# A counting stage of one-hot matrix products: three banks for the counts, one-hots by half batches, a tile's linear products spread over seven slots

## What is computed

```
edge_index = jnp.stack([src, dst])
x = x + _L0_gnn_ref(_layernorm(x), edge_index, L0_gnn_Ws, L0_gnn_Wb, L0_gnn_a_w, L0_gnn_a_b)
x = x + _L0_ffn_ref(_layernorm(x)[None], L0_ffn_Wg, L0_ffn_bg, L0_ffn_We, L0_ffn_be)[0]
x = x + _L1_gnn_ref(_layernorm(x), edge_index, L1_gnn_W, L1_gnn_b)
x = x + _L1_ffn_ref(_layernorm(x)[None], L1_ffn_Wr, L1_ffn_br, L1_ffn_W1, L1_ffn_b1, L1_ffn_W2, L1_ffn_b2)[0]
```

```
Wx = x @ Ws[h] + Wb[h]
s = Wx[v_tgt] @ a_w[h, :d] + Wx[v_src] @ a_w[h, d:] + a_b[h]
alpha = _segment_softmax(leaky_relu(s, 0.2), v_tgt, n)
out_h = segment_sum(alpha[:, None] * Wx[v_src], v_tgt)
```

## Time and profile before

| | us |
|---|---|
| median of 3 runs | 609.81 |
| lowest and highest | 604.17, 610.58 |
| the profiled execution: its time | 610.48 |
| the profiled execution: its span | 608.7 |

### The profile page before, as it was taken

The page is one execution under the profiler, slowest core; times in us unless marked ns, Lnnn a source line. Parts: engine busy times, 40 slices in busy tenths (PEclk is TensorE's granted clock), DMA queues, the critical chain, the costliest instruction groups (busy, mean ns, idle before and its releaser), DMA issues.

```text
span 608.7 us, 11871 instructions
## 1 busy us (share of the span) xinstructions
PE 519.3 (85%) x4561; PEld 369.7 (61%) x4562; DVE 458.2 (75%) x863; ACT 333.0 (55%) x644; POOL 72.5 (12%) x83
## 2 busy tenths in 40 slices
PE   2879999887657998999889478996999965999995
PEld 1856666554457888889777344543466635776762
DVE  6788887788589999996888837785656554687771
ACT  5355555455597999997465433344322217665640
POOL 3000000000000000000000300223132430042252
PEclk9769999999969999999999878999899976899999
DMA  7950000002001111110000067000001039366211
GB/s 190 357 209 1 2 2 1 1 2 90 3 1 44 45 46 45 49 42 2 2 1 2 0 218 283 1 0 0 4 20 54 36 105 381 136 207 208 79 49 47
DMA packets 25304, 45.11 MB, mean 74 GB/s; under 512 B 6961, under 2 KB 7205, under 8 KB 25248
## 3 DMA queue, kind: packets, MB, share of 16 engines
q1 hardware_dynamic: 23264, 39.16, 18.9%
q0 software_dynamic: 1952, 5.18, 2.3%
q10 hardware_dynamic: 32, 0.01, 0.0%
HBM read 33.23 MB, written 11.95 MB: 74 GB/s over the span
## 4 chain that ended last, share of the span: by engine, by line
PE 49%; DVE 25%; issue 13%; ACT 7%; POOL 3%; DMA 1%; ACTq 1%; POOLq 0%; DVEq 0%
PE bank L1300 8%; PE bank L1633 7%; PE bank L1621 6%; PE bank L1364 6%; PE bank L1323 4%; DVE work L1013 4%; PE bank L1371 3%; PE bank L1543 2%; ACT mid L523 2%; PE bank L1478 2%; PE bank L1465 2%; PE bank L1278 2%; DVE rings L1013 2%; POOL row L467 2%; DVE work L971 1%
## 5 line engine op out<-in xcount | busy, mean ns | idle before, releaser
L908 DVE TENSOR_TENSOR big<-mid 128x3072 f16<-128x3072 f16 (+3 forms) x52 | 88.3, 1743 | 9.1 <-PE bank L1371 9.0
L1364 PE MATMUL bank<-big 128*128 128x160 f16 x552 | 72.8, 245 | 13.4 <-ACT mid L523 4.7
L1465 PE MATMUL bank<-big,work 128*128 128x130 f16 x1080 | 67.2, 223 | 12.1 <-DVE work L1013 11.8
L1465 PEld LDWEIGHTS bank<-big,work 128*128 128x128 f16 x1080 | 63.5, 99 | 14.9 <-DVE work L1013 8.1
L1364 PEld LDWEIGHTS bank<-big 128*128 128x128 f16 x552 | 44.3, 105 | 35.1 <-issue 28.0
L1543 PE MATMUL bank<-mid 128*128 128x512 f16 x200 | 47.6, 389 | 3.3 <-POOL mid L441 3.3
L523 ACT ACTIVATE mid<-bank 128x160 f32 x92 | 27.9, 303 | 40.5 <-PE bank L1371 40.4
L625 ACT ACTIVATE mid<-aux,small 128x1280 f16<-128x1280 f32 x36 | 47.4, 1350 | 1.5 <-DVE work L1013 1.1
L1478 PE MATMUL bank<-big,mid 128*128 128x260 f16 x400 | 47.1, 275 | 0.1
L523 ACT ACTIVATE big<-bank 128x160 f32 x92 | 27.9, 303 | 31.6 <-PE bank L1371 29.1
L1478 PEld LDWEIGHTS bank<-big,mid 128*128 128x128 f16 x400 | 38.2, 96 | 7.5 <-issue 0.3
(11 more groups left out here) (293 smaller groups left out, 1100.1 us busy)
## 6 DMA issues: line engine op xcount, KB each, us to landing
big<-in_L_ffn_W SPq DMA_DIRECT2D x10, 1024.0 KB, 9.4
mid<-in_L_ffn_W SPq DMA_DIRECT2D x6, 1024.0 KB, 13.5
xperm_scratch<-work SPq DMA_DIRECT2D x1, 5753.0 KB, 19.4
aux<-thr_scratch SPq DMA_DIRECT2D x8, 640.0 KB, 3.8
aux<-xperm_scratch SPq DMA_DIRECT2D x8, 523.0 KB, 3.9
row<-in_x SPq DMA_DIRECT2D x1, 2304.0 KB
aux<-in_L_gnn_Ws SPq DMA_DIRECT2D x4, 256.0 KB, 4.4
work<-in_L_gnn_W SPq DMA_DIRECT2D x1, 1024.0 KB, 14.8
```

The costliest lines, as they stand in the source:

```text
L908: return V.tensor_tensor(out.rearrange("p c (v two) -> p c v two", two=2), values.rearrange("p (v two) -> p v two", two=2).unsqueeze(1).to ...
L1364: mm(bank[k % 2][:, 0:RW], L_ring[:, slot, k * CH + j, :], R_ring[:, slot, k * CH + j, :], start=j == 0, stop=False)
L1465: ins = mm(acc_region(h, t), weighted[i % NC][:, t * P:(t + 1) * P], VP[:, s, part, h, :, :].rearrange("p b f -> p (b f)"), start=False, s ...
```

## The change

- `count_bank`: the counts of a batch go through three banks, 0, 1 and 7 by (8b + k) % 3, where they went through 0 and 1. count(k+1) then waits for the write of pair k-2, which merge(k) ahead of it has waited for already. merge(k) still waits for the write of pair k-2, since the count matrices are two as before. (Passes after the first, which this input does not have, keep two banks.)
- Bank 7 is given up by the others: tile transposes use bank 6 alone, and `tile_T` of tile t waits for the low half of tile t-1. The weight transposes use banks 6 and 2, and the thresholds 3, 4, 5.
- `half_onehots`: the one-hots of a batch are made in four instructions (1536, 1920, 1536, 1920 elements) where there were two. The first half needs pairs 0 to 3 of batch b-2 counted, the second all eight. `onehots` goes up by 4 behind each half.
- `LIN_SLOTS`: the twelve products stand at k = 0, 1, 3, 4, 5, 6, 7 as 1, 2, 2, 2, 1, 2, 2; none at k = 2, where the transposes are.
- On DVE, `evac_a` goes from the end of iteration t+4 to between the halves of iteration t+5, and `xT_low` from the start of iteration t+4 to the end of t+3.

```
--- before.py
+++ after.py
@@ -54,6 +54,7 @@
 
 
 BEGIN = {1 + t: t for t in range(T)}
+LIN_SLOTS = ((0,), (1, 2), (), (3, 4), (5, 6), (7,), (8, 9), (10, 11))
 B_GW = max(BEGIN) + 2
 B_CS = B_GW + K
 EPS = 1e-5
@@ -291,6 +292,13 @@
                 skip_runtime_bounds_check_because="the groups' windows come from targets in 0 to NP, clipped to the last window")
             return at
 
+        def count_bank(base, k):
+
+            return bank[(0, 1, 7)[(base + k) % 3]] if isinstance(base, int) else bank[k % 2]
+
+        def gw_bank(k):
+            return bank[(6, 2)[k % 2]]
+
         def counts_at(at, k):
 
             return (C, C2)[k % 2][:, :, bass.ds(at, WN)]
@@ -520,7 +528,7 @@
                 for k in range(LB):
                     if not isinstance(base, int):
                         a.wait_ge(sem("counted"), base + (k + 1))
-                    ins = act(counts_at(at[k], k), bank[k % 2][:, 0:RW].rearrange("p (d s) -> p s d", s=T), ACT.Copy)
+                    ins = act(counts_at(at[k], k), count_bank(base, k)[:, 0:RW].rearrange("p (d s) -> p s d", s=T), ACT.Copy)
                     if isinstance(base, int):
                         ins.wait_op(sem("counted"), base + (k + 1), "sem-ge")
                     ins.then_inc(sem("written"), 1)
@@ -576,7 +584,7 @@
                         t = BEGIN[b - 1]
                         if t >= 2:
                             a.wait_ge(sem("linA"), t - 1)
-                        ln_copy(t, bank[6 + t % 2], xTs[:, t % 2, 0, :, :])
+                        ln_copy(t, bank[6], xTs[:, t % 2, 0, :, :])
 
                 write_batch(b * LB, at[b], middle)
                 if b == 0:
@@ -589,11 +597,11 @@
                 if b - B_GW in range(K):
                     k = b - B_GW
                     a.wait_ge(sem("gwT_psum"), k + 1)
-                    act(gWT[:, 0, k, :], bank[6 + k % 2][:, :], ACT.Copy, scale=WS).then_inc(sem("weight_hi"), 1)
+                    act(gWT[:, 0, k, :], gw_bank(k)[:, :], ACT.Copy, scale=WS).then_inc(sem("weight_hi"), 1)
                 if b == B_CS:
                     for i, n in enumerate((4, 4, 2)):
                         a.wait_ge(sem("thrT_psum"), i + 1)
-                        act(thrT[0:H, i * 512:i * 512 + n * P], bank[5 + i][0:H, 0:n * P], ACT.Copy).then_inc(sem("thrT_ready"), 1)
+                        act(thrT[0:H, i * 512:i * 512 + n * P], bank[3 + i][0:H, 0:n * P], ACT.Copy).then_inc(sem("thrT_ready"), 1)
             a.wait_ge(sem("exp_in"), 1)
             act(B12[:, 0, :, :], d1t, ACT.Exp)
             act(B12[:, 1, :, :], d1t, ACT.Exp, scale=SLOPE)
@@ -914,6 +922,14 @@
                 onehot(L_ring[:, slot, :, :], iota_lo, loT[:, bass.ds(off * CH, LC), :], LC, P)
                 onehot(R_ring[:, slot, :, :], iota_q, qT[:, bass.ds(off * CH, LC), :], LC, RW).then_inc(sem("onehots"), LB)
 
+            def half_onehots(b, half):
+                n = LC // 2
+                c = slice(half * n, (half + 1) * n)
+                e = slice(b * LC + half * n, b * LC + (half + 1) * n)
+                at_least(v, "counted", (b - 2) * LB + (half + 1) * (LB // 2))
+                onehot(L_ring[:, b % 2, c, :], iota_lo, loT[:, e, :], n, P)
+                onehot(R_ring[:, b % 2, c, :], iota_q, qT[:, e, :], n, RW).then_inc(sem("onehots"), LB // 2)
+
             def first_onehots():
                 n = LC // 4
                 for q in range(4):
@@ -927,16 +943,18 @@
                     v.wait_ge(sem("ld_x"), 64)
                 if b in BEGIN:
                     ln_stats(BEGIN[b], x[:, BEGIN[b], :])
-                if b - 3 in BEGIN:
-                    t = BEGIN[b - 3]
-                    xT_low(t, bank[6 + t % 2], xTs[:, t % 2, :, :, :])
                 if b - 2 - B_GW in range(K):
                     k = b - 2 - B_GW
                     v.wait_ge(sem("weight_hi"), 2 + k + 1)
-                    V.scalar_tensor_tensor(gWT[:, 1, k, :], bank[6 + k % 2][:, :], WS, gWT[:, 0, k, :],
+                    V.scalar_tensor_tensor(gWT[:, 1, k, :], gw_bank(k)[:, :], WS, gWT[:, 0, k, :],
                                            ALU.mult, ALU.subtract).then_inc(sem("weight_lo"), 1)
                 if b:
-                    onehots(b * LB, b * LB, b % 2, 2)
+                    half_onehots(b, 0)
+                    if b - 4 in BEGIN:
+                        evac_a(BEGIN[b - 4])
+                        if BEGIN[b - 4] == T - 1:
+                            scores()
+                    half_onehots(b, 1)
                 else:
                     first_onehots()
                     passes()
@@ -950,10 +968,9 @@
                                            Wa[:, 0, :, :].rearrange("p k c -> p (k c)"), ALU.mult, ALU.subtract).then_inc(sem("weight_lo"), 1)
                 if b - 1 in BEGIN:
                     ln_scale(BEGIN[b - 1])
-                if b - 3 in BEGIN:
-                    evac_a(BEGIN[b - 3])
-                    if BEGIN[b - 3] == T - 1:
-                        scores()
+                if b - 2 in BEGIN:
+                    t = BEGIN[b - 2]
+                    xT_low(t, bank[6], xTs[:, t % 2, :, :, :])
             exponents()
             v.wait_ge(sem("npass_ready"), 1)
             n = v.value_load(npass[0:1, 0:1], min_val=1, max_val=MAXPASS)
@@ -1310,19 +1327,20 @@
             mm(bank[5][0:NG, 0:1], tri[0:NG, 0:NG], grp[0:NG, 2:3], start=True, stop=True)
             mm(bank[4][0:1, NPAIR:NPAIR + 1], ones[0:NG, 0:1], grp[0:NG, 2:3], start=True, stop=True).then_inc(sem("rb_psum"), 1)
 
-            def lin_a(t, k):
-                if k == 0:
+            def lin_a(t, j):
+                k, i = divmod(j, len(PASSES))
+                xp, wp = PASSES[i]
+                if j == 0:
                     if t == 0:
                         pe.wait_ge(sem("weight_lo"), 2)
                     pe.wait_ge(sem("xT_ready"), t + 1)
                     if t >= 2:
                         pe.wait_ge(sem("evacA"), t - 1)
-                for i, (xp, wp) in enumerate(PASSES):
-                    xt = xTs[:, t % 2, xp, k, :]
-                    start, stop = i == 0 and k == 0, i == 2 and k == K - 1
-                    mm(bank[2 + t % 2][:, :], xt, W016[:, wp, k, :], start=start, stop=stop)
-                    ins = mm(bank[4 + t % 2][:, 0:2 * H], xt, Wa[:, wp, k, :], start=start, stop=stop)
-                if k == K - 1:
+                xt = xTs[:, t % 2, xp, k, :]
+                last = j == K * len(PASSES) - 1
+                mm(bank[2 + t % 2][:, :], xt, W016[:, wp, k, :], start=j == 0, stop=last)
+                ins = mm(bank[4 + t % 2][:, 0:2 * H], xt, Wa[:, wp, k, :], start=j == 0, stop=last)
+                if last:
                     ins.then_inc(sem("linA"), 1)
 
             def second_weights(k):
@@ -1330,10 +1348,12 @@
                 if k == 0:
                     pe.wait_ge(sem("xT_ready"), T)
                     pe.wait_ge(sem("ld_gw"), 16)
+                if k == 1:
+                    pe.wait_ge(sem("evacA"), T - 1)
                 if k >= 2:
                     pe.wait_ge(sem("weight_lo"), 2 + k - 1)
                 for o in range(K):
-                    ins = nc.tensor.transpose(bank[6 + k % 2][:, o * P:(o + 1) * P], gW[:, o, k * P:(k + 1) * P], ident[:, :])
+                    ins = nc.tensor.transpose(gw_bank(k)[:, o * P:(o + 1) * P], gW[:, o, k * P:(k + 1) * P], ident[:, :])
                 ins.then_inc(sem("gwT_psum"), 1)
 
             def thresholds():
@@ -1341,7 +1361,7 @@
                 pe.wait_ge(sem("weight_lo"), 2 + K)
                 for i, n in enumerate((4, 4, 2)):
                     for q in range(n):
-                        ins = nc.tensor.transpose(bank[5 + i][0:H, q * P:(q + 1) * P], thr[:, 4 * i + q, :], ident[:, :])
+                        ins = nc.tensor.transpose(bank[3 + i][0:H, q * P:(q + 1) * P], thr[:, 4 * i + q, :], ident[:, :])
                     ins.then_inc(sem("thrT_psum"), 1)
 
 
@@ -1359,16 +1379,16 @@
 
             def count(base, slot, k):
                 pe.wait_ge(sem("onehots"), base + (k + 1))
-                at_least(pe, "written", base + (k - 1))
+                at_least(pe, "written", base + (k - 2) if isinstance(base, int) else base + (k - 1))
                 for j in range(CH):
-                    mm(bank[k % 2][:, 0:RW], L_ring[:, slot, k * CH + j, :], R_ring[:, slot, k * CH + j, :],
+                    mm(count_bank(base, k)[:, 0:RW], L_ring[:, slot, k * CH + j, :], R_ring[:, slot, k * CH + j, :],
                        start=j == 0, stop=False)
 
             def merge(base, k, at):
 
                 if not isinstance(base, int):
                     pe.wait_ge(sem("written"), base + k - 1)
-                ins = mm(bank[k % 2][:, 0:RW].rearrange("p (d s) -> p s d", s=T), ident16[:, :], counts_at(at[k], k),
+                ins = mm(count_bank(base, k)[:, 0:RW].rearrange("p (d s) -> p s d", s=T), ident16[:, :], counts_at(at[k], k),
                          start=False, stop=True)
```

(9 more changed lines are left out.)

77 lines of the change are left out of this document (48 added, 29 removed).

## The result

| | us |
|---|---|
| before, median of 4 runs beside it | 608.46 (604.17 to 610.58) |
| after, median of 4 runs | 589.74 (588.83 to 591.3) |
| ratio, with its 95% interval | 0.9704, 0.9643 to 0.9764 |
| the profiled execution: time, span | 591.3, 589.5 |

The change makes the kernel about 3% faster. Of all runs in this document one, among the ten of the variant with two banks, fell in a slower state of the chip, and its row leaves it out. I set the trace of after against the same three landmarks as the forecast.

The account below looks back on a forecast made before the run. PE, waiting for its two count banks, was taken to bound the counting stage, with DVE following. Gains of 5.4 and 6.4 us, 11.8 off the profiled 610.5, gave 598.7, stated as 598.5; range 594.5 to 604.5.

Parts of the forecast that it names:

- Batches 0 to 2 I leave as they are: Start of the counting stage, up to batch 3's first merge: no gain entered in the sum.
- 1 or 2 us more: Batches 1 to 3: possible extra gain, as half of batch 2's one-hots no longer wait for batch 0's end.
- Products: Batches 3 to 12, which carry linear products: from 69.8 to 64.4 us, 5.4 us less.
- 0.93 is lost, all in the five slots that have no product: PE in batches 3 to 12: of the 7.04 us period, 0.93 goes to counts waiting for ScalarE to empty the bank.
- DVE follows PE there: Batches 3 to 12: DVE's 6.38 us of work plus a 0.67 wait for PE's products, so PE sets the period.
- These cost nothing while DVE is ahead: Moved `evac_a` and `xT_low` on DVE: no cost; if DVE is not ahead, 6.52 a batch instead of 6.46.
- Rest: From batch 12's last merge to the last count write: from 48.7 to 42.3 us, 6.4 us less.
- The 0.45: Pair loop: at most 0.45 us from the write's start to the merge, giving 0.79 for two pairs, 0.40 for one.
- A: Pair loop not shortened: pairs stay at 0.495 us, PE decides again, 4 us of gain lost, 603 us; chance 0.12.
- B: DVE's fixed part per instruction is 0.16 us: iterations 6.70, one-hots 4.06, 3.4 us lost, 602 us; chance 0.10.
- C: DVE's lead too short: PE waits for `xT_low` every batch, nothing gained with products, 604 us; chance 0.10.
- D: PE's clock falls to 1.2 GHz from its short waits in batches 13 to 22: slower, 616 us; chance 0.06.

Follow-up runs that it names:

- the second pair of series: The changed kernel, unedited, run again beside the kernel before: median 590.59 us, ratio 0.9723.
- the whole hand-over: Changed kernel with its four one-hot instructions handed over together and waiting together for all of batch b-2: 595.8 us, ratio 0.9836.
- the late weight halves: Changed kernel with DVE's four low halves of the third layer's weights moved to the end of iterations 14 to 17: 590.97 us, ratio 0.9735.
- whole one-hots: Changed kernel with DVE's weight halves late, thresholds one batch later, and two one-hot instructions a batch except in batches 2 and 22: 589.91 us, ratio 0.9722.

## Why the prediction missed

**The start (5.2 us, forecast 0): the largest part of the miss.** The step that failed is "Batches 0 to 2 I leave as they are". Two things are in it. About 1.6 is the change, and the three banks' (43.91 with them alone, 45.53 with the rest alone). My text had "1 or 2 us more" in the range, put down to the half batches, and left it out of the sum. About 3.6 is the half-speed stretch, 17.1 us long in the execution on which the sum was made and 3.4 in the one that was profiled after. I read a clock of 0.66 in the earlier trace rows as a property of the kernel; the second execution gave the same, the third a shorter stretch. The runs of the kernel before have a spread of 6 us, and the profiled one, 610.48, was at their upper end. The spread goes loosely with the mean clock (of the runs beside the last four kernels, 604.2 to 604.4 at 0.953 and 609.9 to 610.3 at 0.942 to 0.945, but one of 608.1 at 0.957), and most of it is not the start's: of the 3.1 us between the first and the third profiled execution 0.3 stand ahead of the last merge and 2.8 behind it, where the clock was low for 54.8 and 49.2 us. At equal low clock the last merge moved from 163.63 to 147.90, 15.7 us, and the median of the second pair of series by 1 - 0.9723 of 606.9, 16.8. From 610.5 the forecast's 11.8 should have been 15.7.

**Products (7.0, forecast 5.4).** The number came near on a wrong reading. "0.93 is lost, all in the five slots that have no product" does not fit the rows: four slots have none, and they lose 0.63. The other 0.30 is in slot k = 1, which took 1.37 from the merge at 81.33 to the next, where its three products and the pair need 1.07:

```profile
81.77 0.37 PE L1364 MATMUL bank<-big 128*128 128x160 f16 x3
...
82.70 0.30 PE L1371 MATMUL bank<-mid,ident 128*128 x1
```

That is a wait for the bank too (81.33 to 81.77), and the wait for `xT_low` is hidden under it: `xT_low` ends at 88.93, 0.09 ahead of the product at 89.02. With the banks alone the same slot takes 1.63 and the period is 7.03. "DVE follows PE there" is true, but with the wait for the bank gone PE follows DVE as well. The loop of 7.05 was in rows that I had quoted, with `evac_a` ahead of the statistics and `xT_low` behind them. The change happened to open it ("These cost nothing while DVE is ahead"), an edit that I had counted at nothing and on which most of the term rests: the banks without it gained 1.9 of the 7.0. (No run takes the new order alone out of the changed kernel.) Of the sizes:
- The wait for the normalised tile is 0.27, forecast 0.2.
- The address load costs nothing, forecast 0.15. PE needs 6.11 + 0.27 = 6.38, which is what the merges show (6.46 forecast): 1.0 us in nine batches, as 57.5 stands against 58.5.
- Batch 12 took 5.28, forecast 5.9: two of the twelve products (0.49) stand behind its last merge, and I had counted them in.
- DVE's iteration is 6.42, forecast 6.52.

**Rest (7.0, forecast 6.4).** Here most steps held. The 1.16 from the last merge to the first weight half came out to the hundredth. The half instructions cost what the quarters of batch 0 said:

```profile
120.00 23.33 DVE L916 TENSOR_TENSOR big<-mid 128x1536 f16<-128x1536 f16 x24
```

Six batches in 23.3, 3.9 each where the forecast had 3.88, without a wait in the row. The fixed part that the Trainium skill gives (VectorE: DVE Perf Modes, The TRN2 errata), by which the estimate was 4.05, is not what a further instruction costs here; its page Perfetto Trace Analysis (Optimizing Scalar/DVE Operations) names about 60 ns of an engine's own time per DVE operation, half of what shows as latency, and with that the 0.07 agrees. The last write is 1.74 behind the last half (143.24), forecast 2.2: pairs are 0.35 apart, not 0.40. Rows of PE and ACT at the end of the stage:

```profile
143.60 0.30 PE L1391 MATMUL bank<-mid,ident 128*128 x1
...
143.94 0.30 ACT L531 ACTIVATE mid<-bank 128x160 f32 x1 [0.58 <-PE bank L1391]
...
143.94 0.30 PE L1391 MATMUL bank<-big,ident 128*128 x1
...
144.29 0.31 PE L1391 MATMUL bank<-mid,ident 128*128 x1
```

The write starts 0.34 behind its merge, and the next merge but one can start 0.35 behind that (merge 143.60, write 143.94, merge 144.29). The loop over the count matrices is thus at most 0.69 for two pairs, and PE's own work is 0.68; the rows do not say which of the two decides. The 0.45 that I took from the earlier trace rows was the count's wait, not the merge's.

**The rivals.** A fell (0.35, not 0.495), B fell (0.07), C fell (no wait for `xT_low` in batches 4 to 11). D fell too, for this change: the clock stayed at 1.00 in the stretches from 60 to 95 and from 115.5 to 145, where PE waits in short pieces and cycles through three banks. The rule of the Trainium skill (TensorE: Matmul & The Clock Gate, A second HAM failure mode) that spoke for D thus did not show here. Falls behind 46 us within the counting stage stood in three runs, each about when PE had stood still at once: for 2.11 in every period with the products dealt out alone (five falls, none behind the first of these waits, at 49.3), for 2.70 with the whole hand-over, for 2.41 with the late weight halves. A single wait of 1.81 with whole one-hots had none. That the waits bring the falls is likely from this and not shown; the falls between 23 and 42 us had only one of 1.7 at 20 us close ahead of them, or, in the two kernels with eight matmuls more, not even that.

**The sum.** 5.2 at the start, 1.6 with products and 0.6 in the rest make the 7.4 between 598.7 and 591.3; the profiled execution after is also 1.6 above its median, which with the 0.2 that I had taken off gives 8.8, the distance from 598.5 to 589.74.

## What to carry to other kernels

Before a period is put down to one engine's waits, add up every loop that closes in one period (produce, evacuate, reuse) and compare its length with the period: where two bounds have the same height, either edit alone gains nothing there (banks 7.03, order 7.05), a third makes it worse (10.27), and together, with the half batches and the dealt-out products, they give 6.37. Profile the kernel before more than once: a sum that starts from one execution inherits its clock, and here 3.6 of the 19.2 us between the two profiled executions were that. Compare variants over the stage that was edited, between two of its own landmarks: that repeated within 0.2 us where whole executions spread by 6. An edit that moves steps "at no cost" may be the one on which the others depend, so price what happens if it is left out.

## What the hardware showed that I had not expected

- The clock of TensorE falls to half for 0 to 17.1 us between 23 and 42 us, in executions of one and the same program, while PE has work (busy 19 to 22 of 26 us in every row above). Some 10 us of it cost 3.3 us of time (40.53 against 43.85). A stretch of 3.4 at 28.4 us cost only 0.14 (40.39 against 40.53), one of 3.4 at 32.1, in the kernel with eight matmuls more, 1.6 (41.97).
- In the dealt-out products alone a wait of 2.11 in every 10.27 came with a granted clock of 0.81, while the changed kernel's many waits of up to 0.97 in batches 13 to 22 came with 1.00.
- Two PSUM banks cost 0.15 a pair (0.495 against 0.35), although a count and its merge are only 0.34 long: the way from a merge through ScalarE's write to the next count in the freed bank is 0.79 (148.02 to 148.81 in the earlier trace rows).
- Handing one-hots over in halves is worth nothing in the kernel before and 4.3 us of the stage in the changed one, 3.0 of them in batch 13, where the producer's lead is gone; a part may be the half clock that came with the wait there.
